# A fused adaLN transformer block on one core: shared steps dealt out anew over the four blocks of a batch, TensorE starting a block with the value products

## The reference, cut to what matters

```python
h = _layernorm(x) * (1 + ca) + sa
q, k, v = heads(h @ Wq), heads(h @ Wk), heads(h @ Wv)   # 16 heads of 64
s = einsum('bhid,bhjd->bhij', q * scale, k)
p = where(causal_mask, 0.0, exp(s - max(s)))            # max over the whole row
x = x + ga * ((p @ v / (sum(p) + 1e-8)) @ Wo + bo)
h = _layernorm(x) * (1 + cb) + sb
hidden = silu(fp4(h) @ fp4(w_gate).T) * (fp4(h) @ fp4(w_up).T)
x = x + gb * (fp4(hidden) @ fp4(w_down).T)
```

## Time and profile before

| | |
|---|---|
| median of 3 runs | 1419.69 us (1419.22 to 1420.4) |
| the profiled execution, its own time | 1420.77 us |
| its span, first to last instruction | 1418.8 us |
| granted TensorE clock, mean | 0.982 |
| TensorE products busy | 1268.3 us (89%) |
| TensorE weight loads busy | 1045.9 us (74%) |
| VectorE busy | 1010.3 us (71%) |
| ScalarE busy | 836.0 us (59%) |
| GpSimd busy | 826.5 us (58%) |

### The profile page before, as it was taken

The page is one execution under the profiler, slowest core; times in us unless marked ns, Lnnn a source line. Parts: engine busy times, 40 slices in busy tenths (PEclk is TensorE's granted clock), DMA queues, the critical chain, the costliest instruction groups (busy, mean ns, idle before and its releaser), DMA issues.

```text
span 1418.8 us, 34191 instructions
## 1 busy us (share of the span) xinstructions
PE 1268.3 (89%) x10194; PEld 1045.9 (74%) x10194; DVE 1010.3 (71%) x2565; ACT 836.0 (59%) x2885; POOL 826.5 (58%) x1582
## 2 busy tenths in 40 slices
PE   5989999999999999999999999999999999999963
PEld 3778777777877777877777877777787777787752
DVE  5667777777777777777777777777777777777664
ACT  3666655665655656656666665566566565665630
POOL 2545656655656666655566565665565656665543
PEclk9999999999999999999999999999999999999985
DMA  3000000000000000000000000000000000000000
GB/s 96 16 18 19 8 20 20 17 20 20 4 20 20 17 20 20 7 18 20 20 17 20 19 5 20 20 17 20 20 4 20 20 17 20 20 6 14 18 18 10
DMA packets 38057, 26.54 MB, mean 19 GB/s; under 512 B 2800, under 2 KB 33392, under 8 KB 38032
## 3 DMA queue, kind: packets, MB, share of 16 engines
q1 hardware_dynamic: 38032, 26.23, 6.5%
HBM read 21.94 MB, written 4.28 MB: 18 GB/s over the span
## 4 chain that ended last, share of the span: by engine, by line
POOL 48%; issue 36%; PE 8%; DVE 3%; ACT 2%; POOLq 2%; DMA 1%; SPq 0%; DVEq 0%; ACTq 0%
POOL probs L431 21%; POOL qy L75 6%; POOL qy L73 5%; POOL probs L429 5%; POOL hq L77 3%; PE ps_m L818 2%; POOL rstd L439 2%; POOL h2a L469 2%; POOL xq L77 1%; POOL x_keep L486 1%; POOL x_gb L459 1%; PE ps_s L913 1%; PE ps_o L940 1%; PE ps_m L797 1%; PE ps_m L864 1%
## 5 line engine op out<-in xcount | busy, mean ns | idle before, releaser
L559 ACT ACTIVATE probs<-ps_s,neg_max 128x128 f32<-128x128 f32 (+1 forms) x1024 | 426.0, 432 | 404.9 <-PE ps_s L922 404.9
L431 POOL TENSOR_SCALAR probs<-probs,r_den 128x256 f32<-128x256 f32 (+1 forms) x768 | 341.8, 462 | 0.0
L429 POOL TENSOR_TENSOR probs<-probs,r_den 128x128 f32<-128x128 f32 x256 | 102.5, 400 | 401.8 <-DVE r_den L739 401.8
L730 DVE TENSOR_REDUCE neg_max<-ps_s 128x4 f32<-128x1024 f32 x256 | 304.2, 1219 | 20.2 <-PE ps_s L913 17.2
L656 DVE COPY probs_t<-ps_m 128x512 f32<-128x512 f32 x256 | 176.3, 689 | 134.4 <-PE ps_m L797 134.4
L913 PE MATMUL ps_s<-qk 64*128 64x256 f32 x2048 | 258.3, 391 | 0.4 <-ACT qk L525 0.4
L797 PE MATMUL ps_m<-ident,probs 128*128 128x128 f32 x1536 | 232.4, 274 | 3.9 <-DVE probs_t L656 2.4
L913 PEld LDWEIGHTS ps_s<-qk 64*128 64x128 f32 x2048 | 188.3, 188 | 42.8 <-ACT probs L559 10.9
L559 ACT ACTIVATION_READ_ACCUMULATOR probs<-ps_s,neg_max 128x1 f32 x1024 | 219.2, 214 | 0.0
L940 PE MATMUL ps_o<-probs_t,v 128*64 128x256 f32 (+1 forms) x2048 | 196.0, 333 | 14.3 <-ACT o_t L551 14.3
L940 PEld LDWEIGHTS ps_o<-probs_t,v 128*64 128x64 f32 x2048 | 132.3, 137 | 91.5 <-issue 58.5
(11 more groups left out here) (107 smaller groups left out, 1695.0 us busy)
## 6 DMA issues: line engine op xcount, KB each, us to landing
mod_a<-mod_rows SPq DMA_DIRECT2D x32, 256.0 KB, 3.4
x_in<-L_attn_x SPq DMA_DIRECT2D x32, 128.0 KB, 2.1
x_res<-L_attn_x SPq DMA_DIRECT2D x32, 128.0 KB, 2.1
out<-y_out SPq DMA_DIRECT2D x32, 128.0 KB, 2.9
mod_b<-mod_rows SPq DMA_DIRECT2D x32, 64.0 KB, 3.0
wkv<-L_attn_Wkv SPq DMA_DIRECT2D x2, 512.0 KB, 7.1
wq<-L_attn_Wq SPq DMA_DIRECT2D x1, 512.0 KB, 4.0
wo<-L_attn_Wo SPq DMA_DIRECT2D x1, 512.0 KB, 8.4
```

The lines of the kernel that those rows point to most:

```text
L429: nc.gpsimd.tensor_tensor(cols, cols, r_den[:, u % 4, 0:1].to_broadcast([P, P]), ALU.mult)
L431: ins = nc.gpsimd.tensor_scalar(cols, cols, r_den[:, u % 4, s:s + 1], 1.0, ALU.mult, ALU.mult)
L559: ins = nc.scalar.activation(probs[:, u % 4, h, t * P:(1 + 2 * t) * P], ps_s[:, 2 * (u % 2) + h, t * N:t * N + (1 + t) * P], ACT.Exp, bias ...
L730: nc.vector.tensor_reduce(neg_max[:, u % 4, :], ps_s[:, 2 * (u % 2):2 * (u % 2) + 2, :].rearrange("p b (t j) -> p (b t) j", t=2), AX.X, AL ...
```

## The change

**TensorE** begins a block with `values(j)`, then the two `scores`, then places 0 and 1 (`t0` and `qk0`), then the masks of unit 2j, place 2 (`t1`), the masks of unit 2j+1, and the rest.

**The places.** The table of nine places a block becomes `SHARED`, with 9, 10, 9 and 8 places. Both `wo` steps now end block 1; the `gate`, `up`, `v`, `hqt` and `down` steps are dealt out anew; `t1` stands at place 2 and `t2` at place 6 (block 0) or 5 (the others).

**ScalarE** moves `out_copy` of block 1 from behind the first unit's exponentials to behind the reads of place 5; in the other blocks it stands behind the reads of place 7, ahead of place 8. One wait (`wo_full`) goes. In block 2 the reads of place 4 stand ahead of the second unit's exponentials.

**VectorE** forms the statistics of x1 early in block 2 and the second normalised values in block 2 instead of block 3, does each hidden quantisation (scales and powers of two) behind the reads of place 4, and quantises h2 in block 3 ahead of the reads of places 5 and later, so ahead of both `down` reads.

**GpSimd** rounds the quantised h2 at the end of block 3 instead of behind the first `normalize` of the next block 0, rounds the hidden values in blocks 1 and 3 instead of 2 and 3, ahead of `normalize(2j)`, and does the elementwise steps h2a and h2 in block 2.

```diff
+        SHARED = (
+            ("t0", "qk0", "t1", ("v", 0, 0), ("xqt", 2, 0), "qk1", "t2", ("gate", 2, 0), ("v", 0, 1)),
+            ("t0", "qk0", "t1", ("up", 2, 0), ("gate", 2, 1), "t2", "qk1", ("up", 2, 1), ("wo", 1, 0), ("wo", 1, 1)),
+            ("t0", "qk0", "t1", ("v", 0, 2), ("hqt", 2, 0), "t2", "qk1", ("v", 0, 3), ("xt", -1, 0)),
+            ("t0", "qk0", "t1", ("hqt", 2, 1), "t2", "qk1", ("down", 2, 0), ("down", 2, 1)))
...
-                    if j == 0 and has.prev2:
-                        pool.wait_ge(xq_steps, QUANT_STEPS * (i - 1))
...
-                    if j in (2, 3) and has.prev2:
-                        round_hidden(i - 2, j - 2)
+                    if j in (1, 3) and has.prev2:
+                        round_hidden(i - 2, (j - 1) // 2)
...
+                    if j == 3 and has.prev:
+                        pool.wait_ge(xq_steps, QUANT_STEPS * i)
+                        if has.prev2:
+                            pool.wait_ge(xqt_full, i - 1)
+                        quantize_round(nc.gpsimd, Steps(pool, xq_round, ROUND_STEPS, i - 1), xq, 2 * P // BLOCK, scale[0],
...
-                    if has_out and j == 1:
-                        out_copy()
-                    for n in (0, 1, 2, 3):
+                    first = 5 if j == 2 else 4
+                    for n in range(first):
                         shared_reads(n)
                     if has.attn:
                         exponentials(2 * j + 1, 0)
-                    shared_reads(4)
-                    shared_reads(5)
+                    for n in range(first, 6):
+                        shared_reads(n)
+                    if j == 1 and has.prev:
+                        out_copy()
                     if has.attn:
                         exponentials(2 * j + 1, 1)
-                    for n in (6, 7, 8):
+                    for n in range(6, 8):
                         shared_reads(n)
-                    if has_out and j != 1:
+                    if j != 1 and has.unit(2 * (j - 2)):
                         out_copy()
+                    for n in range(8, len(SHARED[j])):
+                        shared_reads(n)
...
+                    shared_reads(j, 4)
+                    if j == 1 and has.prev2:
+                        hidden_scales(i - 2, 0)
...
+                    if j == 1 and has.prev2:
+                        hidden_magic(i - 2, 0)
...
                 for j in range(PAIRS):
+                    if has.unit(2 * (j - 2)):
+                        values(j)
                     if has.attn:
                         scores(2 * j)
                         scores(2 * j + 1)
-                    if has.unit(2 * (j - 2)):
-                        values(j)
+                    at_place(j, 0)
+                    at_place(j, 1)
                     if has.attn:
                         mask(2 * j, 0)
                         mask(2 * j, 1)
-                    at_place(j, 0)
-                    at_place(j, 1)
+                    at_place(j, 2)
                     if has.attn:
                         mask(2 * j + 1, 0)
                         mask(2 * j + 1, 1)
-                    for n in range(2, 9):
+                    for n in range(3, len(SHARED[j])):
                         at_place(j, n)
```

More of the change, by code:

```diff
@@ L301, in iterations, with place_of @@
                 body(i)
-        PLACES = {
[3 rows of a table removed]
[L308 to L316, removed]
+        SHARED = (
[4 rows of a table added]
+        def place_of(j, step):
+            part = int(step[-1]) if isinstance(step, str) else 0
+            if not isinstance(step, str):
+                return step
+            if step[0] == "t":
+                return ("t", 0, 3 * (j - 1) + part) if j > 0 else ("t", 1, 3 * (PAIRS - 1) + part)
+            return ("qk", 0, 2 * (j + 1) + part) if j < PAIRS - 1 else ("qk", -1, part)
+        PLACES = {(j, n): place_of(j, step) for j in range(PAIRS) for n, step in enumerate(SHARED[j])}
+        assert len(PLACES) % 3 == 0
+        WEIGHT_PLACES = [(0, 7), (1, 3), (1, 4)]
         def shared_steps(i):
@@ L462, in body @@
                         rstd(i + 1, ln1_pool, ln1_steps, LN_STEPS * (i + 2), mv1, var1, rstd1)
-                    if j in (2, 3) and has.prev2:
-                        round_hidden(i - 2, j - 2)
[L465 to L473, removed]
+                    if j == 2 and has.prev:
+                        rstd(i - 1, ln2_pool, x1_steps, X1_STEPS * i, mv2, var2, rstd2)
+                    if j in (1, 3) and has.prev2:
+                        round_hidden(i - 2, (j - 1) // 2)
                     if i_is(i, 0) and j > 0:
@@ L546, in out_copy @@
                     def out_copy():
-                        if j == 2 and has.prev:
-                            act.wait_ge(wo_full, 2 * i)
                         at = 2 * ((j - 2) % PAIRS)
@@ L563, in exponentials @@
                         ins.then_inc(exp_done, 1)
-                    has_out = has.unit(2 * (j - 2))
                     if has.attn:
@@ L752, in body @@
                     shared_reads(j, 0)
+                    if j == 2 and has.prev:
+                        dve.wait_ge(x1_steps, X1_STEPS * (i - 1) + 2)
+                        layer_norm_stats(x1, stats2, mv2, x1_steps, X1_STEPS * (i - 1) + 2)
                     shared_reads(j, 2)
+                    shared_reads(j, 3)
                     if has.attn:
                         denominators(2 * j)
[L756 to L761, removed]
+                    shared_reads(j, 4)
+                    if j == 1 and has.prev2:
+                        hidden_scales(i - 2, 0)
                     if j == 0 and has.next:
@@ L764, in body @@
                         layer_norm_stats(x_in, stats1, mv1, ln1_steps, LN_STEPS * (i + 1))
+                    if j == 1 and has.prev2:
+                        hidden_magic(i - 2, 0)
+                    if j == 2 and has.prev2:
+                        hidden_scales(i - 2, 1)
+                    if j == 2 and has.prev:
+                        dve.wait_ge(ln2_pool, 2 * i)
+                        normalized([xn2[:, t * P:t * P + P] for t in range(2)], x1, mv2, rstd2, xn2_ready)
+                    if j == 2 and has.prev2:
+                        hidden_magic(i - 2, 1)
                     if j == 1 and has.next:
@@ L767, in body @@
                         normalized([xn[:, t, :] for t in range(2)], x_in, mv1, rstd1, xn_ready)
[L768 to L776, removed]
                     if j == 3 and has.prev:
@@ L784, in body @@
                                        inverse[0], qy[0], qm[0])
+                    for n in range(5, len(SHARED[j])):
+                        shared_reads(j, n)
                     if j == 3 and i_is(i, -1):
```

13 lines of the change are left out of this document (8 added, 5 removed), and 3 rows, old and new, of the table PLACES.

## The result

| | before | after |
|---|---|---|
| median | 1419.69 us | 1612.14 us (1610.10 to 1615.59) |
| ratio, 95% interval | | 1.1357 (1.133 to 1.1385) |
| profiled execution, its own time | 1420.77 us | 1610.10 us |
| span | 1418.8 us | 1608.0 us |
| one iteration, steady | 42.10 us | 48.12 us |

A fourth execution of the kernel before took 1489.27 us, 4.9% over the median of the other three, and is left out of its median and of the ratio as a slow run.

What follows compares the result with a forecast made beforehand. TensorE was taken as the bound before; after, a loop through masks, ScalarE and its out copy. Thirty iterations at 4.95 (148 us), plus 11 at the start, less 3 in the tail: 1576 us, range 1541 to 1611.

Steps and rivals of the forecast that it cites:

- Sum 47.05 us against 42.10: All four blocks of one iteration, 11.21, 12.93, 11.79 and 11.12 us: 4.95 us more per iteration than before.
- Two `wo`, 3.40: TensorE at the end of block 1: two steps, one taken as 1.70 us, in a block of 12.93 us.
- The low part of h, 0.41: VectorE in block 3: forms it behind the first maximum in 0.41 us, over at 4.23 us; qk0 waits for it.
- `t0`, 0.35: TensorE: a group of transposes ahead of qk0 and the masks, 0.35 us of the 4.52 us from values to masks.
- The clock: A rival weighed on its own and left out of the range; chance 4%.
- ScalarE's 0.19 us for `qk1` in block 0: ScalarE in block 0: TensorE's qk1 ends at 8.1 us and is readable 0.2 later, so ScalarE waits 0.19 us.
- The error of up to 0.5 us a block: Waits of 0.2 to 0.5 us a block missed or doubled, up to 1 us an iteration: 35 us either way.
- The tail's gain: End of the kernel: the tail's quantisation no longer stands behind `down`, 3 us back.
- the late start of the loop: Iterations 0 and 1: the loop exists only from block 2 of iteration 0, with fewer copies; estimated 11 us.
- values wait for the copy: Sign on TensorE: wait for ScalarE's out copy of 1.3, 1.9 and 0.8 us at ends of blocks 0, 2, 3.
- place 4 waits: Sign on TensorE: place 4 waits for ScalarE to read `qk`, about 1 us in every block.
- GpSimd's own rival: Block 1: hidden rounding and normalize, over near 15.8 us, delay `t0` of block 2, wanted at 16.3; 1607 us, chance 10%.

Runs made afterwards that it cites:

- scores_first_round_first: The change with TensorE's old order (scores, values, masks early) and GpSimd's block-3 hidden rounding ahead of normalize of unit 5: 1365.73 us, ratio 0.9615.
- h_low_early: The change, with VectorE forming the low part of h ahead of both maxima of block 3 instead of between them: 1595.68 us, ratio 1.1238.
- qk_read_early: The change, with ScalarE reading place 1 (qk0) ahead of the first unit's exponentials: 1591.96 us, ratio 1.1226.
- hidden_round_first: The change, with GpSimd's hidden rounding in block 3 ahead of normalize of unit 5 instead of behind it: 1597.02 us, ratio 1.1254.

## Why the prediction was wrong, and where it was right

Wrong is the size: +192 us measured, +156 forecast, and 1612.14 lies 1.1 us above the range. Direction and mechanism held, and the runs bear them out: the path from values over masks and ScalarE back to the out copy sets blocks 0, 2 and 3, TensorE sets block 1.

Where the 189 us between the two profiled executions lie, counted from value products to value products: 10.6 us up to iteration 2 (11 forecast), 188 over the thirty iterations with the loop (148 forecast), and 9 given back in the tail (3 forecast). The step that failed is "Sum 47.05 us against 42.10": the thirty iterations. In it:

- **Two `wo`, 3.40.** They took 3.74 us:

```profile
806.62 0.75 PE L827 MATMUL ps_m<-wgu_r,xq_r 128*128 128x352 f32 x3
807.20 3.81 PE L873 MATMUL ps_m<-wo,o_t 128*128 128x128 f32 x32
810.94 1.52 PE L949 MATMUL ps_o<-probs_t,v 128*64 128x256 f32 x16
```

  The 1.70 of the earlier trace rows was a short case. From product to product it is 0.112 us in both kernels, so sixteen are 1.79, and there the next step began only 0.03 us behind the sixteenth. Here thirty-two are 3.57, the second product came 0.07 late, and values 0.09. That is 0.34 of the 1.07 us missing per iteration.
- **The low part of h, 0.41.** It took 0.75, with GpSimd beside it: block 3 came out 0.35 longer. The row of before was true, but another engine's work came to lie beside the step; the forecast looked only at when GpSimd's work ends, and in block 3 not at the rounding at all.
- **`t0`, 0.35.** Behind scores it took 0.41 (787.67 to 790.01 less 1.93 for the scores), behind masks 0.35, and that in blocks 0, 1 and 2 (in block 3 the wait for h covers it); in block 0 the exponentials also came 0.41 behind the masks instead of 0.32. Block 0 came out 0.17, block 2 0.14 and block 1 0.41 (with the `wo`) above the forecast.
- **The clock.** I had given it 4% as a rival on its own. It came as a small thing inside the main case, 6 iterations at 0.9 to 1.3 us, some 6 us in all, each with a fall to a granted clock of 0.50 for 3.4 us. An event that strikes one iteration in five belongs into the range.

4.95 + 1.07 make 6.02 us an iteration; thirty of them are 181, and 6 of the clock make most of 188. The iterations of the kernel before are not alike to the hundredth, as I had written, but last 42.10 to 42.16 us from number 5 on; that changes nothing here. One wait does not follow from its own figures: ScalarE's 0.19 us for `qk1` in block 0 (8.1 + 0.2 - 8.16 is 0.14; the rows show 0.17). The error of up to 0.5 us a block that I allowed for was right in size, but all four blocks erred the same way: `wo` and `t0` were read where their neighbours made them short, and the low part of h where no rounding ran beside it. The tail's gain and the late start of the loop had the right sign.

Of the signs named in advance: the period was to be 47.0 and is 48.12; masks 4.59 us after the start (4.5); values wait for the copy 1.12 us at block 0's end, 1.84 at block 2's and 0.74 at block 3's (1.3, 1.9, 0.8); place 4 waits 0.6 to 1.2 us for `qk`; block 1 has no copy wait; the wait for the maxima has gone. TensorE's products kept the written order: nothing behind values starts before them in any of the rows, also not in the 1.84 us for which values wait at block 2's end, and the periods of the ten kernels lie within 1.4 us of forecasts that build on it. GpSimd's own rival did not come: in block 1 its rounding and normalisation end 0.6 us earlier than TensorE wants `t0`, as worked out.

## What to carry to other kernels

Where one engine's order is turned, follow the path from its first wait over the other engines back to that same wait, and add up one round: a wait that stood behind 1.9 us of independent work cost 0.45 us, and the same wait in front of it 3.7 us an iteration, though every engine was idle 18% or more. Put the instruction that waits for a far-off result behind work that does not, and the instruction that another engine waits for ahead of such work. When costing, take a step's duration from the row that has the same neighbours, on its own engine and beside it, and let the range lean towards longer.

## What was not expected of the hardware

**VectorE steps took up to three times as long beside GpSimd steps.** The subtraction that forms the low part of h took 0.41 to 0.42 us with no rounding step beside it, 0.75 beside an 0.79 us rounding step, 0.86 in scores_first_round_first; over the whole kernel the change has VectorE busy 98 us longer for the same instructions. The largest part is 41 us in the normalised values `xn` of block 1 (median 0.35 to 1.02 us a step), now beside the hidden rounding; the row maxima (304 us in both) and the copies of transposed probabilities out of PSUM (176 us before, 168 in the change) did not grow. In the same iteration, two steps of the hidden quantisation of 0.34 us before took 0.75 and 0.77 beside GpSimd's h2 steps:

```profile
820.14 0.94 POOL L484 TENSOR_TENSOR h2a<-xn,mod_a 128x256 f32<-128x256 f32 x1 [0.22 <-DVE xn L711]
820.53 0.75 DVE L65 TENSOR_SCALAR qm<-qy 128x352 int32<-128x352 int32 x1
821.16 0.72 POOL L488 TENSOR_TENSOR h<-h2a,mod_a 128x256 f32<-128x256 f32 x1
821.32 0.77 DVE L66 TENSOR_SCALAR qm<-qm 128x352 f32<-128x352 f32 x1
```

Each ends some 0.2 us after the GpSimd step that ran when it began. What ties the two engines together no trace here shows. In the kernel before, the subtraction of 720.66 took its 0.41 us beside GpSimd's normalising steps, and those took 1.51 us instead of 1.28; there GpSimd seems to have paid:

```profile
709.82 1.28 POOL L431 TENSOR_SCALAR probs<-probs,r_den 128x256 f32<-128x256 f32 x3
...
720.26 1.51 POOL L431 TENSOR_SCALAR probs<-probs,r_den 128x256 f32<-128x256 f32 x3
```

**The clock can fall after pauses of under 2 us, and need not.** TensorE's wait for the maxima in the kernel before, 1.6 us in iterations 4 to 30, did not lower it: the granted clock is 1.00 from 36 to 1366 us. From iteration 3 to 30, behind one and the same wait of 1.84 us, block 3 had the low clock (0.50 for 3.4 us) in 5 of the 28 iterations of the change, in 10 with h_low_early, in 20 with qk_read_early and in none with hidden_round_first; once that pause held transposes, in none either. What decides it from iteration to iteration these runs do not settle.
